# Naming ScalarE's table sets in a macaron Mamba kernel, with the sines moved behind the exponentials

## What is computed

```python
z, xBC, dt_raw = jnp.split(x @ in_proj_w.T, [D_INNER, 2 * D_INNER + 2 * D_STATE], axis=-1)
xBC = silu(causal convolution of 4 taps over xBC)      # u, Bm, Cm; Bm and Cm normalized
dt = jax.nn.softplus(dt_raw + dt_bias)
A = jnp.exp(A_log)
def step(carry, inp):                                  # one token
    S = 1.0 / (1.0 + dt_t ** 2 * A)
    w = S * (w - dt * A * ys + dt * Bu)
    ys = ys + dt * w
    o = einsum(ys, C_t)
out = (o + D * u) * jax.nn.silu(z) @ out_proj_w.T
```

## Time and profile before

| | |
|---|---|
| runs of the kernel before | 786.61, 892.56 and 2213.87 us, median 892.56 us |
| span of the profiled execution, first to last instruction | 783.3 us |
| lowest run less that span | 3.3 us |
| mean granted TensorE clock | 0.922 |
| busy: PE, DVE, ACT, POOL | 644.3, 547.1, 424.9, 520.4 us |
| ScalarE in the mixer | from 238.66 us on; 66 of its 68 table loads lie there |

### The profile page before, as it was taken

How to read it: one execution, slowest core, us unless ns; L and a number is a source line. 1 busy time by engine, 2 the same in 40 slices (tenths; PEclk the granted TensorE clock), 3 DMA queues, 4 the chain that set the end, 5 groups by cost and what they waited for, 6 DMA issues and landing times.

```text
span 783.3 us, 13708 instructions
## 1 busy us (share of the span) xinstructions
PE 644.3 (82%) x3768; PEld 475.4 (61%) x3768; DVE 547.1 (70%) x1706; ACT 424.9 (54%) x745; POOL 520.4 (66%) x656
## 2 busy tenths in 40 slices
PE   3478979999916288989999998999968999999950
PEld 2245558888812045656575756577635667888840
DVE  4666756666539659897989999999743645666637
ACT  1122225455406999998999998764212324545525
POOL 3787775666645676896978869686765713666660
PEclk9989989999966678999999999999988999999995
DMA  9411223333242000000000000000000212333219
GB/s 266 159 46 52 82 67 80 93 89 85 65 142 84 0 1 1 0 2 1 1 2 1 2 15 15 14 15 15 28 27 28 69 45 76 87 89 91 81 30 318
DMA packets 49368, 46.34 MB, mean 59 GB/s; under 512 B 8456, under 2 KB 42861, under 8 KB 49296
## 3 DMA queue, kind: packets, MB, share of 16 engines
q1 hardware_dynamic: 40592, 28.54, 13.0%
q0 software_dynamic: 8704, 16.93, 6.7%
HBM read 25.30 MB, written 21.19 MB: 59 GB/s over the span
## 4 chain that ended last, share of the span: by engine, by line
PE 35%; POOL 24%; issue 15%; DVE 13%; ACT 8%; DMA 4%; POOLq 1%; SPq 0%; DVEq 0%; ACTq 0%
POOL ys L726 11%; POOL xs L710 10%; PE ps_tr L1662 4%; PE ps_go L1662 3%; DMA xs<-rows,pos 2%; PE ps_tr L2064 2%; PE ps_go L2012 2%; PE ps_go L2051 1%; PE ps_go L1833 1%; PE ps_tr L1850 1%; PE ps_go L1837 1%; POOL rstd L700 1%; PE ps_b L1884 1%; PE ps_a L2002 1%; PE ps_go L1883 1%
## 5 line engine op out<-in xcount | busy, mean ns | idle before, releaser
L726 POOL DMA_INDIRECT ys<-arena,dest x144 | 141.0, 980 | 99.8 <-issue 65.4
L710 POOL DMA_INDIRECT xs<-rows,pos x128 | 127.2, 993 | 58.8 <-issue 35.8
L1006 ACT ACTIVATE silu_a<-ps_a 128x512 f32<-128x512 f32 x32 | 19.1, 597 | 62.1 <-PE ps_a L2002 62.1
L2064 PE MATMUL ps_tr<-w_down_e,arena 128*128 x384 | 50.7, 275 | 0.0
L1521 DVE TENSOR_TENSOR hid<-silu_a,ps_a 128x512 f32<-128x512 f32 x36 | 24.8, 688 | 34.1 <-ACT silu_a L1026 34.1
L1521 DVE TENSOR_TENSOR hid<-silu_a,ps_b 128x512 f32<-128x512 f32 x36 | 24.8, 688 | 34.1 <-ACT silu_a L1026 34.1
L2064 PEld LDWEIGHTS ps_tr<-w_down_e,arena 128*128 128x128 f32 x384 | 46.7, 192 | 0.0
L1035 ACT ACTIVATE arena<-ps_go 128x512 f32<-128x512 f32 x72 | 42.6, 592 | 2.0 <-PE ps_go L2051 2.0
L1488 DVE TENSOR_TENSOR hid<-silu_a,ps_b 128x512 f32<-128x512 f32 x32 | 21.9, 686 | 31.0 <-PE ps_b L2004 29.1
L2051 PE MATMUL ps_go<-ident,hid 128*128 128x128 f32 x288 | 43.2, 273 | 0.2
L1026 ACT ACTIVATE silu_a<-ps_a 128x512 f32<-128x512 f32 x36 | 21.5, 597 | 38.1 <-PE ps_a L2040 38.1
(11 more groups left out here) (368 smaller groups left out, 2032.5 us busy)
## 6 DMA issues: line engine op xcount, KB each, us to landing
arena<-xs SPq DMA_DIRECT2D x144, 65.0 KB, 1.9
rows<-ys SPq DMA_DIRECT2D x8, 512.0 KB, 3.7
arena<-ys SPq DMA_DIRECT2D x8, 512.0 KB, 6.8
ys<-arena,dest POOLq DMA_INDIRECT x144
x<-in_L_attn_x SPq DMA_DIRECT2D x8, 256.0 KB, 4.4
arena<-in_L_ffn_ew SPq DMA_DIRECT2D x4, 512.0 KB, 6.9
xs<-rows,pos POOLq DMA_INDIRECT x128
out<-x SPq DMA_DIRECT2D x8, 256.0 KB, 4.7
```

The source lines that it names most:

```text
L710: pool.indirect_dma_start(xs, bass.IndirectOffsetOnAxis(pos[:, n, i:i + 1], 0), rows[:, n * TT + i % TT, :], None).then_inc(scattered, 16)
L726: pool.indirect_dma_start(ys, bass.IndirectOffsetOnAxis(dest[:, i:i + 1], 0), y_out[:, p % YRING, j, :], None, bounds_check=2 * TOK - 1, o ...
L2064: r = pe.matmul(ps_answers(p)[:, j * P:(j + 1) * P], hid_t[:, p % 2, at:at + P], w_down_e[:, bass.ds(which[2 * p + j], 1), k, :].rearrange ...
```

## The change

Three edits, all in ScalarE's mixer:

```diff
+            def exp_ln_set(at):
+
+                if at(-5) or at(-4):
+                    act.preload_act_table_set("natural_log_exp_and_others")
+
+            def silu_sin_set(at):
+
+                if at(-6):
+                    act.preload_act_table_set("silu_and_others")
+
             def body(at):
                 do(theta, at(-5))
                 do(hnt_copy, at(-8))
                 do(root, at(-5))
+                do(inverse_ln, at(-5))
+                do(inverse_exp, at(-5))
+                silu_sin_set(at)
                 do(sine_c, at(-6))
                 do(h_start, at(-7))
                 do(sine_b, at(-6))
-                do(inverse_ln, at(-5))
-                do(inverse_exp, at(-5))
                 do(silu_gate, at(-8), 0)
...
                 do(arctan, at(-5))
+                exp_ln_set(at)
                 do(zt_copy, at(-4))
                 do(decays, at(-5))
```

## The result

The changed kernel takes 779.11 us (median of six runs, 776.77 to 780.84). The kernel before took 785.39, 786.61 and 787.26 us in its fast runs, which are the ones compared; its other three took 892.56, 2213.87 and 2214.21 us, and no trace shows why. The ratio is 0.9915 [0.9889, 0.9941], 6 to 7 us less: within 2%, and clear of zero. Two later measurements of the same kernel beside the one before gave 0.9933 [0.991, 0.9955] and 0.9914 [0.9889, 0.9939].

What follows compares the result with a forecast made beforehand. ScalarE bounds the fill; TensorE, lastly with VectorE, sets the pace in the full pipeline. Span 783.3 - 7.5 (fill) + 2.5 (load ahead of the copy) = 778.3 us; 3.3 more gives 781.6, said as 782; range 770 to 791.

Steps and rivals of the forecast that it cites:

- Who waits for whom: Mixer: ScalarE fills the pipeline; once full, ScalarE is nearly full but not late, and TensorE, lastly with VectorE, sets the pace.
- fill, to the load of block 1's arctangent: Blocks 0 and 1 of the mixer: fewer loads end the second z projection sooner, 7.5 us gained, bounds 2.7 and 14.2.
- turns of blocks 4 to 6, the load ahead of the copy: Load ahead of `zt_copy` delays TensorE's dt projection: 1.0, 1.3 and 0.2 us, together 2.5 lost, bounds 0 and 8.5.
- Full pipeline: Mixer once filled: the five loads removed per block are worth nothing, hidden by TensorE's own 34.8 us of work.
- The second rival: Fill: GpSimd works without a gap up to L636, so 2.7 us gained, 2.5 lost; 786.4 us, chance 0.14.
- one step of the forecast: Fill: `arctan` must wait for GpSimd's `angle_in` (L636), starting at 260.85 instead of 264.38, 3.5 us sooner.
- block 6 0.2: Block 6, TensorE's dt projection: the load ahead of the input copy was to cost 0.2 us.
- The terms put at nothing: Blocks 2, 3 and 7, waiting for VectorE anyway, and the tail and rest: no gain or loss, 0 us.
- The slower rival: dt projection: the new wait cools TensorE's clock, 3.1 us in each of six blocks; 798 or 805 us, chance 0.04.
- The upper end of the two terms: Smallest fill gain, 2.7 us, with the largest cost of the load ahead of the copy, 8.5: 792 us.
- The estimate by the page's price: At the skill's 2.66 us per switch the fill gives some 10 us, the moved load takes some 6: about 783.

Runs made afterwards that it cites:

- fill-only kernel: The changed kernel with the old order and no named loads from block 2's turn on, 57 loads: 778.03 us, ratio 0.9898 to the kernel before.

## What held of the prediction, and which of its steps failed

The forecast was 782 us, about 5 less than before; measured are 779.1 and 6 to 7 less. Who waits for whom came as forecast. The sum did not: one term was mis-sized, three were put at nothing and were not, and these errors partly cancel. By the profiled executions, in us:

| term of the span's sum | forecast | measured |
|---|---|---|
| fill, to the load of block 1's arctangent | -7.5 | -7.4 |
| turns of blocks 2 and 3 | 0 | -2.5 |
| turns of blocks 4 to 6, the load ahead of the copy | +2.5 | +3.5 |
| turn of block 7 | 0 | 0.0 |
| from there to the last matmuls of `outputs` | 0 | +1.6 |
| rest of the program | 0 | -1.3 |
| span | 778.3 | 777.2 |

**Fill: right step by step, in part by luck.** Starts in us, from the rows of both sides:

| step | before | forecast | changed |
|---|---|---|---|
| ln of block 0, L859 | 249.18 | 246.46 | 246.50 |
| GpSimd's `bc_conv`, L544 | 251.61 | 248.9 | 248.94 |
| first arctangent, L899 | 264.38 | 260.85 | 260.25 |
| input copy of block 1, L814 | 265.80 | 263.6 | 263.09 |
| ln of block 1, L859 | 272.10 | 268.3 | 267.76 |
| `c_places`, L943 | 284.51 | 278.0 | 277.96 |
| silu of block 1, L821 | 288.39 | 281.5 | 281.68 |
| end of the second z projection | 291.8 | 284.2 | 284.6 |

(The prediction read 291.6 us for the end before; the row gives 289.89 + 1.91 = 291.8.) The arctangent's load of block 1 starts at 285.62 and not 292.99: 7.4 us, where 7.5 were forecast. Of these, 1.3 us came without any edit in another execution of the old fill, whose second z projection ran at full speed. The prediction saw that the row of before was at the low clock, and took the full speed for a gain of the change. Two small errors cancel besides: the steps up to the ln of block 1 came 0.5 us sooner than thought, with L544 at 2.95 us and not 4.62, and the projections from L1668 to z took 10.05 us and not 9.52. Forty loads at 1.28 us are 51 us, and ten of them lay in this stretch; what decided was who waited for whom.

**Full pipeline: right that its loads are worth nothing**, by the fill-only kernel. The second rival (GpSimd lets only 2.7 us through) is wrong as a bound, though GpSimd does hold the first arctangent for 2.32 us, as one step of the forecast said.

**The load ahead of the copy: the term that failed, in size and in cause.** The waits came as forecast (a new row of 6.6 us, where five to seven were written). The forecast said 1.0, 1.3 and 0.2 us for blocks 4, 5 and 6; measured are 1.00, 1.42 and 1.04, 3.5 and not 2.5 in all. The largest miss is "block 6 0.2": the wait for the copy is 0.3 us there, but 0.6 us for VectorE's us are new beside it. And with the load behind the copy only 1.2 of the 3.5 us came back. The forecast took the load as the sole cost of the new order in the full pipeline, and VectorE as fixed; VectorE got longer.

**The terms put at nothing.** Blocks 2 and 3 were to gain and lose nothing, as they wait for VectorE anyway; they are 2.5 us shorter, with the clock at 0.95 and 1.00 for 0.86 and 0.95. The tail was to be nothing; it is 1.6 us longer, 46.49 us at a mean clock of 0.89 against 44.84 at 0.92, with the same waits. Neither can be put down to the change: another execution of the changed kernel has the two turns at 32.65 and 37.05 us (before, 32.81 and 36.70), and the tail at 44.51 us and a clock of 1.00. What the sum lacked is a term for the clock: each of these stretches differs by 1 to 2 us between two executions of one kernel, the shorter at the higher clock.

**The slower rival** needed a wait of 1.3 us alone to bring the clock down. It does not: the three turns from 317.11 us on hold waits of 1.6, 1.6 and 1.2 us, and each has 1.00. In that it was rightly held unlikely. That the clock differs between executions all the same, the terms above show.

**The absolute number.** The profiled executions of the changed kernel have a time 1.9 us above their span, three times (779.09 and 777.2, 777.63 and 775.7, 780.74 and 778.9). The forecast used 3.3 us, from a run and a span of before that were not one execution. That is 1.4 of the 2.9 us by which 782 is too high; 1.1 are the span, 777.2 for 778.3, and 0.4 the rounding. The upper end of the two terms, 792 us, lies just outside the stated range of 770 to 791, though the prediction says that the range takes it in.

**The drain.** The Trainium skill, "ScalarE: Activation LUTs", section "What ACT_TABLE_LOAD costs", adds a drain to each switch. The changed kernel agrees with its 1283 ns and again shows no drain: L883 ends at 252.70 us and the load starts at 252.72. The estimate by the page's price, about 783, is 4 us above the measured 779.1. The time alone could not have told it from the forecast of 782; the rows do.

## What to carry to other kernels

Count a table load only where another engine waits behind it: some ten of these forty were worth 6 to 7 us, the others nothing, and a single one moved ahead of a copy that TensorE needs made it wait 0.3 to 1.6 us a block. Ask that anew for each stage, since an engine that bounds the fill may be idle a quarter of the time in the full pipeline. And when a wait is to be removed, check what stands right behind it: in blocks 4 to 6 the waits for the copy were 3.1 us, and taking them away gave back 1.2. And before a microsecond in one profile is put down to an edit, look at the granted clock of the stretch in a second execution: here it moved single stretches by up to 2 us.

## What the runs showed of the hardware

**A small VectorE instruction can last as long as the GpSimd instruction beside it.** VectorE, then GpSimd, in the changed kernel, blocks 5 and 6:

```profile
399.00 1.24 DVE L1165 TENSOR_SCALAR bc_n<-bc_n 128x8 f32<-128x8 f32 x1
...
434.97 1.20 DVE L1437 CAST top_f<-top_i 128x8 f32<-128x8 uint32 x1
```
```profile
398.75 1.46 POOL L632 TENSOR_TENSOR hid<-hid 128x512 f32<-128x512 f32 x1
...
434.84 1.30 POOL L632 TENSOR_TENSOR arena<-arena 128x512 f32<-128x512 f32 x1
```

Before, the same two instructions took:

```profile
407.83 0.16 DVE L1153 TENSOR_SCALAR bc_n<-bc_n 128x8 f32<-128x8 f32 x1
...
442.39 0.17 DVE L1425 CAST top_f<-top_i 128x8 f32<-128x8 uint32 x1
```

Both start just after GpSimd's L632 and end within 0.03 us of its end (400.24 and 400.21, 436.17 and 436.14). Before, the first of them fell into a gap of GpSimd's, between 407.62 and 408.30 us. ScalarE's softplus now comes sooner, GpSimd's `dt_sum` with it, and so it meets other instructions of VectorE. In block 6 this one instruction is 1.03 us of the 1.06 by which VectorE's busy time grew, and TensorE waits 0.6 us for VectorE's us later in that turn. With the load behind the copy from block 4 on, it is the instruction just ahead of that cast that meets GpSimd's L632 (434.94 to 436.21 us); it took 0.15 us before:

```profile
434.95 1.28 DVE L1438 TENSOR_TENSOR gap<-top 128x4 f32<-128x4 f32 x1
```

In block 4 of both kernels it is an update of the state (L1292 in the changed kernel, 128x256), 1.60 us long for 0.49 before, also beside L632. So in each of these three turns one instruction has grown by 1.0 to 1.1 us, wherever the load stands. The Trainium skill, "SBUF — State Buffer", section "Who interferes with whom", has VectorE and GpSimd share a port pair: a VectorE instruction in a mode that uses two ports, which the page says `tensor_scalar` and `cast` can enter, contends with GpSimd, and the one that issues first holds the pair for its whole instruction while the other is blocked. These rows agree, GpSimd being first both times. That this makes up the 2.3 us which the load's place does not explain fits these rows, but no experiment moved GpSimd's L632 to show it.

**The granted clock differed between executions of one kernel**: in blocks 2 and 3 it was 0.95 and 1.00 in one profile of the changed kernel, 0.90 and 0.95 in another, 1.2 and 1.5 us of time; in the tail 0.89 and 1.00, 46.49 and 44.51 us. What decides it stays open.
